# Row norms as products with an indicator, and split products in the query features, in an attention and mixture kernel on one core

## The reference

```python
def softmax_kernel(x, proj, is_query):
    norm = x.shape[-1] ** (-0.25)
    ratio = proj.shape[0] ** (-0.5)
    xp = jnp.einsum('bhnd,md->bhnm', x * norm, proj)
    diag = jnp.sum(jnp.square(x), axis=-1, keepdims=True) * 0.5 * (norm * norm)
    if is_query:
        stab = jnp.max(xp, axis=-1, keepdims=True)
    else:
        stab = jnp.max(xp, axis=(-1, -2), keepdims=True)
    return ratio * (jnp.exp(xp - diag - stab) + EPS_K)
```

## Time and profile before

| | us |
|---|---|
| median of 3 runs | 796.31 |
| span of the profiled execution | 795.2 |
| TensorE products, busy | 726.8 (91%) |
| TensorE weight loads, busy | 596.6 (75%) |
| VectorE | 617.5 (78%) |
| ScalarE | 470.8 (59%) |
| GpSimd | 367.7 (46%) |

### The profile page before, as it was taken

One profiled execution on the slowest core, in us unless ns is written; L12 is line 12 of the kernel. 1 busy time (PEld: TensorE's weight loads), 2 busy tenths in 40 slices (PEclk: granted clock), 3 DMA queues, 4 the chain that ended last, 5 costly groups with the idle time before them and its releaser, 6 DMA issues. The chain is left out here.

```text
span 795.2 us, 16192 instructions
## 1 busy us (share of the span) xinstructions
PE 726.8 (91%) x6012; PEld 596.6 (75%) x6012; DVE 617.5 (78%) x1298; ACT 470.8 (59%) x749; POOL 367.7 (46%) x358
## 2 busy tenths in 40 slices
PE   8998999999999999999999979975899999999950
PEld 7867768768768768768768758865788889998850
DVE  5877778978878888888788787888867677677683
ACT  4655736867867867867857834464145544455470
POOL 4364316526527517517517512501344466445563
PEclk9899999999999999999999999999699999999985
DMA  8100010011011011011011011250256654556593
GB/s 244 37 2 2 1 54 2 27 54 56 28 54 54 26 53 54 26 53 54 26 53 29 28 54 55 59 191 0 81 187 146 160 149 96 126 153 167 127 267 115
DMA packets 51184, 62.60 MB, mean 79 GB/s; under 512 B 9408, under 2 KB 44992, under 8 KB 51136
## 3 DMA queue, kind: packets, MB, share of 16 engines
q1 hardware_dynamic: 44016, 49.74, 19.5%
q0 software_dynamic: 6864, 12.19, 8.1%
q10 hardware_dynamic: 256, 0.03, 0.0%
HBM read 40.85 MB, written 21.10 MB: 78 GB/s over the span
## 5 line engine op out<-in xcount | busy, mean ns | idle before, releaser
L2153 PE MATMUL pF<-w,h 128*128 128x256 f32 x448 | 106.0, 382 | 0.0
L2153 PEld LDWEIGHTS pF<-w,h 128*128 128x128 f32 x448 | 81.8, 190 | 13.2 <-issue 3.4
L893 ACT ACTIVATE h<-pX,b1cur 128x512 f32<-128x512 f32 x64 | 44.3, 692 | 61.9 <-DVE b1cur L1925 46.5
L1128 POOL DMA_INDIRECT kp<-row_scratch,idx_g x32 | 41.3, 1291 | 80.5 <-DVE idx_g L1825 56.5
L982 POOL TENSOR_SCALAR ve<-mv 128x4 f32<-128x4 f32 x36 | 8.5, 236 | 141.4 <-DVE mv L1205 140.5
L2584 PE MATMUL pX<-w_lo,h_hi 128*128 128x256 f32 x256 | 73.9, 288 | 0.0
L2584 PE MATMUL pX<-w_hi,h_lo 128*128 128x256 f32 x256 | 72.4, 283 | 0.0
L2584 PE MATMUL pX<-w_hi,h_hi 128*128 128x256 f32 x256 | 72.4, 283 | 0.0
L1883 DVE TENSOR_TENSOR h_lo<-h,h_hi 128x512 fp32r<-128x512 f32 x64 | 42.9, 690 | 27.0 <-ACT h_hi L885 26.3
L1136 POOL DMA_INDIRECT acc_scratch<-qp,idx_s x28 | 53.4, 1907 | 22.5 <-DVE qp L1862 18.3
L1305 DVE RECIPROCAL den<-den 128x512 f32<-128x512 f32 x14 | 46.9, 3348 | 7.5 <-ACT den L541 7.5
(11 more groups left out here) (427 smaller groups left out, 2149.5 us busy)
## 6 DMA issues: line engine op xcount, KB each, us to landing
kp<-fc1T SPq DMA_DIRECT2D x8, 1024.0 KB, 7.6
w<-fc2T SPq DMA_DIRECT2D x8, 1024.0 KB
xin<-video SPq DMA_DIRECT2D x7, 512.0 KB, 3.8
x<-video SPq DMA_DIRECT2D x7, 512.0 KB, 4.5
out<-x SPq DMA_DIRECT2D x7, 512.0 KB, 3.0
acc_scratch<-xf SPq DMA_DIRECT2D x7, 512.0 KB, 2.9
row_scratch<-y SPq DMA_DIRECT2D x7, 512.0 KB, 3.0
kp<-acc_scratch SPq DMA_DIRECT2D x4, 512.0 KB, 6.0
```

The source lines that it names most:

```text
L893: nc.scalar.activation(h[:, n, :], pM[n % M_SLOTS], ACT.Gelu_apprx_tanh, bias=b1cur[:, n:n + 1]).then_inc(he_ready, 1)
L1128: pool.indirect_dma_start(xg[:, g, :], None, row_d, bass.IndirectOffsetOnAxis(ap=idx_g[:, g:g + 1], axis=0)).then_inc(gathered, 16)
L2153: ins = nc.tensor.matmul(pF[m][:, half * D:(half + 1) * D], h[:, k, tok(2 * m + half)], w2[:, k, :], start=(k == 0), stop=(k == FC - 1))
```

## The change

Four things change.

- **Row norms of K.** The transposes of kT, their squares and the sums on VectorE go. ScalarE squares kT as it lies (`k_squares`, one instruction of 128x1024), and TensorE multiplies the squares with the indicator `of_16`, which says which 16 features belong to a head (`norms_of_keys`: for each of four token tiles and two groups one float32 product, squares stationary, 8 columns moving). VectorE scales the 64 columns out of pA into dgk.
- **Row norms of Q.** They are made in the same way from the squares of qT (`norms_of_queries`, ahead of `ff_out(0, 0)`) and added to the row tops in `tops_with_norms`, so that norms and tops are turned together.
- **The projection of Q** in `features_turned` becomes three split products (`projbd_hi`, `projbd_lo`, `q_hi`, `q_lo`).
- **The tops.** High part and rest lie in different rows of one operand, `mxT`, and one selector product takes both. The two products with the squares go.

`turn_kmax` and `spread_kmax` move ahead by one and two steps, `rest_of_queries` stands later in VectorE's order than `rest_of_squares` did, and the indicators take a few more small instructions before batch 0.

The core of the diff, indented less:

```diff
@@ -58,10 +58,11 @@
+Q_STEPS = TT + 1
-(J_K, J_Q, J_V, J_DK, J_ST, J_CTX, J_KSUM, J_CTXT, J_DEN, J_OUT, J_WO) = (
-    0, 2, 4, 6, 8, 10, 11, 12, 13, 15, 17)
+(J_K, J_Q, J_V, J_DK, J_ST, J_DQ, J_CTX, J_KSUM, J_CTXT, J_DEN, J_OUT, J_WO) = (
+    0, 2, 4, 6, 7, 9, 10, 11, 12, 13, 15, 17)
@@ -160,11 +161,13 @@
-selc = sb("selc", [P, 2, M], F32R)
+projbd_hi, projbd_lo = sb("projbd_hi", [P, 2 * M], F32R), sb("projbd_lo", [P, 2 * M], F32R)
+of_rest = sb("of_rest", [P, 4])
+rest_rows = sb("rest_rows", [P, 1])
@@ -178,8 +181,10 @@
-qsq_lo = sb("qsq_lo", [P, G, N], F32R)
-mxT_hi, mxT_lo = sb("mxT_hi", [P, N], F32R), sb("mxT_lo", [P, N], F32R)
+q_lo = sb("q_lo", [P, G, N], F32R)
+mxT_hi, mxT = sb("mxT_hi", [P, N], F32R), sb("mxT", [P, N], F32R)
+mxq, dgq = (qe[:].rearrange("p a b -> p (a b)")[:, 2 * N + k * TT * H:2 * N + (k + 1) * TT * H].rearrange("p (t h) -> p t h", t=TT)
+            for k in range(2))
@@ -576,10 +581,10 @@
-    def squares(i, m):
-        wait(act, dg_ready, i * 2 + m - 1)
-        take_a(i, J_DK + m, sq[:, m % 2].rearrange("p a b -> p (a b)"), ACT.Square, sq_ready)
+    def k_squares(i):
+        act.wait_ge(kT_ready, (i + 1) * G)
+        nc.scalar.activation(sq[:].rearrange("p a b d -> p (a b d)"), kT.rearrange("p g n -> p (g n)"), ACT.Square).then_inc(sq_ready, 1)
@@ -607,8 +612,7 @@
         nc.scalar.activation(qsqT, qT[:], ACT.Square).then_inc(qsq_ready, 1)
-        act.wait_ge(qsq_ready, i * 2 + 1)
-        nc.scalar.activation(qsq_hi[:], qsqT, ACT.Copy).then_inc(qsq_ready, 1)
+        nc.scalar.activation(q_hi[:], qT[:], ACT.Copy).then_inc(qsq_ready, 1)
@@ -670,8 +674,7 @@
-        squares(0, 0)
-        squares(0, 1)
+        k_squares(0)
@@ -708,8 +711,7 @@
-            squares(i, 0)
-            squares(i, 1)
+            k_squares(i)
@@ -1234,17 +1235,16 @@
-    def norms(i, m, dg):
-        dve.wait_ge(sq_ready, i * 2 + m + 1)
-        nc.vector.tensor_reduce(dg[:, 2 * m:2 * m + 2, :], sq[:, m].rearrange("p a (h d) -> p a h d", d=DH), AX_X,
-                                ALU.add).then_inc(dg_ready, 1)
+    def norms(i, job, dg):
+        dve.wait_ge(a_ready, i * A_JOBS + job + 1)
+        nc.vector.tensor_scalar(dg.rearrange("p t h -> p (t h)"), pA[job % 2][:, 0:TT * H], 0.5 * NORM * NORM, None, ALU.mult).then_inc(dg_ready, 1)
-        nc.vector.scalar_tensor_tensor(
-            out=kbias[:], in0=dgk[:], scalar=0.5 * NORM * NORM, in1=pA[(J_ST + 1) % 2][:, 0:H].unsqueeze(1).to_broadcast([P, TT, H]),
-            op0=ALU.mult, op1=ALU.add).then_inc(kbias_ready, 1)
+        nc.vector.tensor_tensor(kbias[:], dgk[:], pA[(J_ST + 1) % 2][:, 0:H].unsqueeze(1).to_broadcast([P, TT, H]),
+                                ALU.add).then_inc(kbias_ready, 1)
@@ -1273,21 +1273,30 @@
-    def rest_of_squares(i):
+    def rest_of_queries(i):
-        nc.vector.tensor_tensor(qsq_lo[:], qsqT, qsq_hi[:].bitcast(F32), ALU.subtract).then_inc(ql_ready, 1)
+        nc.vector.tensor_tensor(q_lo[:], qT[:], q_hi[:].bitcast(F32), ALU.subtract).then_inc(ql_ready, 1)
-        nc.vector.tensor_tensor(mxT_lo[:], pXall[:, 0, :], mxT_hi[:].bitcast(F32), ALU.subtract).then_inc(ql_ready, 1)
+        nc.vector.scalar_tensor_tensor(out=mxT[:], in0=pXall[:, 0, :], scalar=rest_rows[:, 0:1], in1=mxT_hi[:].bitcast(F32),
+                                       op0=ALU.mult, op1=ALU.add).then_inc(ql_ready, 1)
-        nc.vector.tensor_reduce(mxp[:, t, :].rearrange("p (a r) -> p a r", a=4)[:, :, 0:4],
+        nc.vector.tensor_reduce(mxq[:, t, :].rearrange("p (a r) -> p a r", a=4),
+    def tops_with_norms(i):
+        dve.wait_ge(qmx_ready, i * Q_STEPS + TT)
+        dve.wait_ge(dg_ready, (i + 1) * 2)
+        tops, halves = (a.rearrange("p t (a r) -> p (t a) r", r=4).unsqueeze(2).to_broadcast([P, TT * 4, 2, 4]) for a in (mxq, dgq))
+        nc.vector.tensor_tensor(mxp.rearrange("p t (a x r) -> p (t a) x r", a=4, r=4)[:, :, 0:2], tops, halves,
+                                ALU.add).then_inc(qmx_ready, 1)
@@ -1364,17 +1373,16 @@
+        norms(0, J_DK, dgk[:])
-        norms(0, 0, dgk)
-        norms(0, 1, dgk)
-        rest_of_squares(0)
-        dve.wait_ge(dg_ready, 2)
+        rest_of_queries(0)
+        dve.wait_ge(dg_ready, 1)
@@ -1383,6 +1391,8 @@
         q_max(0, 3)
+        norms(0, J_DQ, dgq)
+        tops_with_norms(0)
@@ -1434,27 +1444,27 @@
             k_max(i, 1)
-            norms(i, 0, dgk)
-            norms(i, 1, dgk)
+            norms(i, J_DK, dgk[:])
             q_max(i, 0)
+            k_top(i, sa)
             q_max(i, 1)
-            k_top(i, sa)
-            rest_of_squares(i)
-            dve.wait_ge(dg_ready, (i + 1) * 2)
+            dve.wait_ge(dg_ready, i * 2 + 1)
             q_max(i, 3)
+            norms(i, J_DQ, dgq)
+            tops_with_norms(i)
+            rest_of_queries(i)
@@ -1509,8 +1519,13 @@
-    nc.vector.tensor_scalar(selc[:], of_half[:].unsqueeze(2).to_broadcast([P, 2, M]), -0.5 * NORM * NORM, None, ALU.mult)
-    nc.vector.tensor_scalar(selm[:].rearrange("p g k m -> p (g k) m"), of_head[:].unsqueeze(2).to_broadcast([P, 2 * G, M]), -1.0, None, ALU.mult)
+    built.link(nc.vector.tensor_reduce(of_rest[:], ident[:].rearrange("p (a r) -> p r a", a=4)[:, 4:8], AX_X, ALU.add))
+    built.link(nc.vector.tensor_reduce(rest_rows[:], of_rest[:], AX_X, ALU.add))
+    built.link(nc.vector.tensor_scalar(rest_rows[:], rest_rows[:], -1.0, None, ALU.mult))
+    built.link(nc.vector.tensor_tensor(of_head[:], of_rest[:], of_head[:], ALU.subtract))
+    nc.vector.tensor_copy(selm[:].rearrange("p g k m -> p (g k) m"), of_head[:].unsqueeze(2).to_broadcast([P, 2 * G, M]))
+    built.link(nc.vector.tensor_copy(projbd_hi[:], projbd[:]))
+    nc.vector.tensor_tensor(projbd_lo[:], projbd[:], projbd_hi[:].bitcast(F32), ALU.subtract)
@@ -1999,7 +2014,7 @@
-               + [(v_ready, 2, m) for m in range(2)] + [(sq_ready, 2, m) for m in range(2)] + [(stab_ready, 1, 0), (kbias_ready, 1, 0)] + [(cs_ready, 2, m) for m in range(2)]
+               + [(v_ready, 2, m) for m in range(2)] + [(dg_ready, 2, 0), (stab_ready, 1, 0), (kbias_ready, 1, 0), (dg_ready, 2, 1)] + [(cs_ready, 2, m) for m in range(2)]
@@ -2050,7 +2065,7 @@
-            pe.wait_ge(qmx_ready, i * TT + 2 * (n - J_XQ))
+            pe.wait_ge(qmx_ready, i * Q_STEPS + 2 * (n - J_XQ))
@@ -2102,13 +2117,22 @@
-    def turn_heads(i, m, src):
-        s = slot_a(i, J_DK + m)
-        for t2 in range(2):
+    def norms(i, job, squares):
+        s = slot_a(i, job)
+        for t in range(TT):
-                cols = s[:, t2 * D:(t2 + 1) * D].rearrange("p (a g x) -> p g a x", a=4, g=G)[:, g]
-                ins = turn(cols, src[:, g, tok(2 * (m % 2) + t2)])
+                dst = s[:, t * H:(t + 1) * H].rearrange("p (a g k) -> p g a k", a=4, g=G)[:, g]
+                ins = nc.tensor.matmul(dst, squares[:, g, tok(t)], of_16[:].rearrange("p (a k) -> p a k", a=4), start=True, stop=True)
+    def norms_of_keys(i):
+        pe.wait_ge(sq_ready, i + 1)
+        norms(i, J_DK, sq[:].rearrange("p a b d -> p (a b d)").rearrange("p (g n) -> p g n", g=G))
+    def norms_of_queries(i):
+        pe.wait_ge(qsq_ready, i * 2 + 1)
+        norms(i, J_DQ, qsqT)
@@ -2176,6 +2200,7 @@
+            pe.wait_ge(qmx_ready, (i + 1) * Q_STEPS)
@@ -2183,11 +2208,8 @@
-            if g == 0:
-                pe.wait_ge(qsq_ready, (i + 1) * 2)
-            parts = ((projbd[:], qT[:, g, :]), (selc[:].rearrange("p k m -> p (k m)"), qsq_hi[:, g, :]),
-                     (selc[:].rearrange("p k m -> p (k m)"), qsq_lo[:, g, :]),
-                     (selm[:, g].rearrange("p k m -> p (k m)"), mxT_hi[:]), (selm[:, g].rearrange("p k m -> p (k m)"), mxT_lo[:]))
+            parts = ((projbd_lo[:], q_hi[:, g, :]), (projbd_hi[:], q_lo[:, g, :]), (projbd_hi[:], q_hi[:, g, :]),
+                     (selm[:, g].rearrange("p k m -> p (k m)"), mxT[:]))
@@ -2322,8 +2344,8 @@
             values(1)
-            turn_heads(0, 0, kT)
-            turn_heads(0, 1, kT)
+            first_batch(proj_ready, 3)
+            norms_of_keys(0)
@@ -2332,6 +2354,7 @@
             fold_of_hidden(4, FC)
+            norms_of_queries(0)
@@ -2354,8 +2377,7 @@
             values(1)
-            turn_heads(i, 0, kT)
-            turn_heads(i, 1, kT)
+            norms_of_keys(i)
@@ -2387,16 +2408,20 @@
             hidden(4)
+        if att:
+            turn_kmax()
+        if ff:
         if att:
-            turn_kmax()
+            spread_kmax()
             features(i, J_XQ + 1, qT, 1)
-            spread_kmax()
             hidden(7)
+        if att:
+            norms_of_queries(i)
```

More of the change, by code:

```diff
@@ L289, in build @@
             aT_lo = early("aT_lo", [P, C, N], F32R)
-            qsq_hi = early("qsq_hi", [P, G, N], F32R)
+            q_hi = early("q_hi", [P, G, N], F32R)
             qT = early("qT", [P, G, N])
```

## The result

The changed kernel takes 842.42 us in the median of four runs (836.84 to 850.17), against 796.14 before: 46 us slower. The ratio of 1.056 (95% interval 1.0535 to 1.0583) is taken without the longest run, which counts as slow. The profile is that of this longest run (850.17, span 848.4). Its clock was low for longer than that of the others: worked out from each run's span and mean granted clock, TensorE was at half clock for some 106 us in it, and for 75, 86 and 89 us in the other three (estimates).

What follows compares the result with a forecast made beforehand. TensorE, busy 58.01 of 58.85 us a batch, was taken as the bound. Batch terms of 27.9, 2.65 and 1.4 us gave 828.3, and 17 for the clock gave 845 (836 to 854; 8 in 10: 822 to 861).

Steps and rivals of the forecast that it cites:

- The wait: TensorE idles before the norms of K until ScalarE's square, queued behind two copies, ends: 3.05 us a batch, batches 2 to 7.
- Norms of K: 8 transposes (0.85 us) go, 16 float32 records at 0.114 us come, 1.8 us: net +0.95 a batch.
- Norms of Q: Before ff_out(0, 0), 16 float32 records are added and nothing is removed: +1.8 us a batch, no wait.
- Features: features_turned, twice a batch: four split parts in place of one float32 and four split parts, -0.85 us each.
- Tails: Waits before context (idle put at 0.4 us) and for GpSimd's sums at sums_of_keys: together +0.35 us a batch (0 to 0.8).
- The sum without the clock: Batches 2 to 7 +27.9 us, batch 1 +2.65, batch 0 +1.4: 828.3 us before any clock fall.
- The clock: Half clock around wait and sparse norms: 2.5 us for each of batches 2 to 7, 2 for batches 0 and 1 together.
- the clock did not hold: Rival: the wait is there but TensorE's clock holds at full speed, 828 us (822 to 834); chance 0.15.
- the products are not priced by columns: Rival: norms products cost by streamed columns, 0.03 us a record in place of 0.114, 807 to 824 us; chance 0.07.
- no later product passed the waiting ones: Rival: later products pass the waiting ones in TensorE's queue, hiding wait and norms behind hidden(0); faster, 788 us; chance 0.03.
- The rival with longer falls: Rival: the clock falls for 6.8 us each time, and again around the norms of Q, 856 to 864 us; chance 0.12.

Runs made afterwards that it cites:

- the squares early: The changed kernel with ScalarE's square of kT moved ahead in its program in every batch; 805.73 us.
- the doubled products: The changed kernel with ScalarE's square of kT moved ahead, and each norms product of K and Q issued twice in a row; 866.91 us.
- the filler in the wait: The changed kernel with filler products of 128 columns on TensorE where it waits for the squares of K; 824.66 us.

## Why the prediction was right

845 was forecast and 842.4 measured. That they lie within 3 us of each other is in part luck, as four runs of the kernel spread over 13. Term by term, for batches 2 to 7 at first:

- *The wait*, 3.05 us: 3.00. The step that carried the case was to ask what stands ahead of the square in ScalarE's program.
- *Norms of K*, 1.8 for 16 records: 1.80 with the squares early. *Norms of Q*, 1.8: 1.70, from 298.61 to 300.31. The price by the record of the earlier trace rows held, and the doubled products confirm it: 0.11 us for 8 columns, about what a transpose with 128 takes. That the load of the weights is what costs it was argued; no run separates the load from another fixed cost.
- *Features*, -0.85 each: the first split part takes 0.34 us and the others 0.23, as the earlier trace rows said.
- *Tails*: the idle time in front of `context` is 0.36, forecast 0.4. In the sum of 0.35 GpSimd's share was the larger, and little of it shows: that is part of why the whole came to 4.4 a batch (63.23 - 58.83, with the filler in the wait) and not 4.65.
- *The sum without the clock*, 828.3: the kernel with the filler gives 824.7. Batches 2 to 7 gave 26.4 us in place of 27.9, batch 1 gave 2.3 for 2.65 and batch 0 0.8 for 1.4.
- *The clock*, +17 as an estimate between 0 and 27: 17.8 in the medians, and 12 to 25 in the single runs. The mechanism held, but how the term was divided did not. In the profiled execution, where the clock cost 25, batches 2 to 7 took 13.3 us of it, 2.2 each, where I had 2.5; batch 0 alone took some 9.6 (10.4 longer, against 0.8 with the filler), where I had given batches 0 and 1 together 2. So batch 0 is mis-sized at least there: behind its wait follow products of one column and fillers in small number, and the clock stayed low through them. How the 17.8 of the median divide, no trace shows.

What I had as rivals fell: the clock did not hold, the products are not priced by columns, and no later product passed the waiting ones. The rival with longer falls was right for batches 0, 2 and 3 only.

What stays open: what exactly the clock answers to in the changed kernel. In batches 2 and 3 it fell within the wait, before any sparse product, so there the wait behind `key_features(0)` was enough. In batches 4 to 7 it fell only with the sparse products under way or just done. Together the two lowered it in every batch; the sparse products alone (1.8 us) in one of 14 groups, twice as many of them in 13 of 14. The wait without norms behind it wasn't tried.

## What to carry to other kernels

Before a producer is moved to another engine, read that engine's program order at the new place: the wait is as long as what stands in front of the producer, and it is paid in full where the consumer bounds the kernel. A product with 8 moving columns cost as much here as one with 128, 0.11 us a record, so replacing transposes and sums by it pays only if the other engine was the bound. And a saving on the busiest engine counts only up to the next chain that ends beside it; look for work to put there, and take the pieces large enough, since every cut costs too.

## What the runs showed of the hardware

TensorE's clock fell without any idle time. In the kernel with the doubled products, rows of 3.6 us of products that stream 8 columns per 0.11 us lowered it in 13 of 14 groups, 2.0 to 4.7 us after the first of them, and within 7 us it was back. In the changed kernel it also fell with TensorE idle, 1.95 and 2.68 us into the waits of 3.0 us in batches 2 and 3. With the wait filled by products of 128 columns it held in all batches from 1 to 7. The Trainium skill ("TensorE: Matmul & The Clock Gate", "HAM oscillation — how this bites in real kernels") describes the idle gap as the cause; the falls within the waits of batches 2 and 3 agree with that, and the kernel with the doubled products shows that a busy TensorE isn't enough. And at half clock the records of the norms doubled too, from 0.11 to 0.21 us.
